# Routing tokens to expert slots by scatters and gathers of whole token rows, beside a sequential scan, on one Trainium2 core

## The chip, the cores and the metric

One core of one Trainium2 chip runs the whole program. The metric is the device time of one execution in microseconds, and less is better. The engines are TensorE (PE), VectorE (DVE), ScalarE (ACT), GpSimd (POOL) and SyncE (SP), which here only issues DMAs. A time comes from several runs; the profile is of one more execution.

## The reference

The input `x` is 4 sequences of 1024 tokens with 256 features, float32. After a layer norm, two branches read `xn`:

```python
# branch 1: a recurrence over the 1024 time steps, state h of (4, 256, 16)
dt = soft_clamp(softplus(xn @ Wdt.T + bdt), 0.001, 0.1, 0.5)
def step(h, inp):
    h = dAt * h + dBt * xt[..., None]
    h_norm = sqrt(sum(h * h, axis=(1, 2)))          # per sequence
    h = h * minimum(20.0 / (h_norm + 1e-08), 1.0)
    y = einsum('bdn,bn->bd', h, Ct) + Dp * xt
# branch 2: a mixture of 8 experts, top 2, capacity 1280 slots an expert
top_v, top_i = top_k(xn @ w_g, 2)
rank = cumsum(one_hot(top_i))                        # a token's place in its expert
keep = rank < 1280
exp_batches = einsum('tec,td->ecd', sec_mask, xn)    # token rows to their slots
exp_out = gelu(exp_batches @ c_fc) @ c_proj          # 256 -> 1024 -> 256
moe = cb_weight @ exp_out                            # back, weighted by softmax of the two
out = x + s * silu(moe)                              # s: output of branch 1
```

## The kernel before

**The scan.** DVE runs the 1024 steps one after the other, lines 778 to 811: the decayed state `vv` (L778), the clamp argument (L781), two reductions (L784, L792), a sum over partitions (L796), the new state `hr` (L807) and the recurrence of the norm (L811). In each step POOL takes one power (L554, `scale_of`) that L807 of the step needs and L781 has released. The state of all four sequences lies in one 128x128 tile a step.

**What feeds the scan.** Four steps are a quad, sixteen a block, 64 a half, so that a half is 16 quads. For each quad PE transposes four decay columns (L1227), ACT takes them out (L1009), PE spreads the inputs of four steps (L1231) and ACT takes these out with a scale (L1016). `da`, `ur` and `hr` are rings of 32 steps, so PE and ACT may run at most about two blocks ahead; they start a block when DVE has finished the block before the last. For each half ACT prepares the decays of the next: 32 tanhs (L912, `tanh_ops`, two a quad) and then four exponentials of 128x2048 (L919, `decay_ops`), which PE awaits at the head of a half (`decay_ready`). DVE also prepares input of later halves in pieces put between steps by the tables `sum_at` (`add_logs`, L637), `input_at` (`scan_input`, L645) and `norm_at` (L652). They are put one step behind a step with an indirect DMA (`delayed`), nine pieces a half.

**The experts.** 10240 slots are 40 tiles of 256, five an expert. A tile is one `turn` (four transposes of gathered rows), four `up` (8 matmuls each and one Gelu) and two `down` (16 each). A list `by_quad` spreads this work evenly over quads 1 to 231, by weights 1, 4 and 8. Rows of a tile are fetched from `xnd` in DRAM by two indirect gathers (L529) through the list `slot_src`, and its results are written to `moe` by two indirect scatters (L534) through `slot_dst`. POOL issues these at the steps of the table `at_step`, between two powers. ACT may overwrite `yrow` when POOL has seen the scatters land (`yrow_free`, a step of `freed_at`). From quad 240 on, PE combines: SP loads `moe` in token order (`load_pair`), ACT makes diagonal weights, PE adds the two rows and ACT takes the Silu.

**The prologue.** For eight tiles of the 4 x 128 tokens DVE normalizes; SP stores `xn` to `xnd`, `xn * Dp` to `dx` and the transposed tile to `xts`; PE makes the logits. `dxn` is a double buffer, so the tile after next waits for a store to `dx` to land. Then DVE works out experts, ranks and weights (L680 to L722), and one-hot products on DVE, POOL and PE invert the token-to-slot map into the slot lists (`one_hot`, `moe_rows`, `slots`, L731, L737, L520, L1146). The semaphore `loop_go` holds all engines until this is over:

```python
            pool.sem_inc(loop_go, 1)
            pool.wait_ge(loop_go, 5)
```

All of SP's DMAs stand in one queue, in order.

Of the kernel before, what the change touches and what calls it, by code (L numbers as in the profile page):

```python
# [20 lines left out]
P = 128  # L21
# [27 lines left out]
CONSTS = 22  # L49


def build(nc, x, wdtT, bdt, wb, wc, a_log, dpar, w_g, c_fc, c_proj, out):
# [4 lines left out]
    with ctx:  # L57
# [7 lines left out]
        xnd = nc.dram_tensor("xnd", (TOK + P, D), f32, kind="Internal").ap()  # L65

        moe = nc.dram_tensor("moe", (2 * TOK + P, D), f32, kind="Internal").ap()
# [21 lines left out]
        slot_src = sb("slot_src", [P, SC + EC], i32)  # L89
        slot_dst = sb("slot_dst", [P, SC], i32)  # L90
# [53 lines left out]
        def lay(n):  # L144
            at2[0] += n
            assert at2[0] <= 34688, at2[0]
            return arena[:, at2[0] - n:at2[0]]

        dxn = lay(2 * NB * D).rearrange("p (f b d) -> p f b d", f=2, b=NB)
# [21 lines left out]
        lo = lay(2 * JT).rearrange("p (k j) -> p k j", k=2)  # L171
        hi = lay(2 * JT).rearrange("p (k j) -> p k j", k=2)
        rank_i = lay(2 * JT).bitcast(i32).rearrange("p (k j) -> p k j", k=2)
        lo_i = lay(2 * JT).bitcast(i32).rearrange("p (k j) -> p k j", k=2)
        hi_i = lay(2 * JT).bitcast(i32).rearrange("p (k j) -> p k j", k=2)
        rowid = lay(2 * JT).rearrange("p (k j) -> p k j", k=2)
        rowid_i = lay(2 * JT).bitcast(i32).rearrange("p (k j) -> p k j", k=2)
        cols_i = lay(P).bitcast(i32)
        cols = lay(P)
        pcol = lay(1)  # L180
        acc = lay(SC)
        free = lay(SC)

        lohot = wp.rearrange("p k d -> p (k d)").rearrange("p (f n c) -> p f n c", f=2, n=8)
        wflat = wf.rearrange("p k d -> p (k d)")
        hihot = wflat[:, 0:8 * SC].rearrange("p (n c) -> p n c", n=8)
        hirow = wflat[:, 8 * SC:24 * SC].rearrange("p (f n c) -> p f n c", f=2, n=8)
        pw = lay(4 * JT).rearrange("p (k j) -> p k j", k=4)
        alog = lay(DH * NS)


# [56 lines left out]
        lo_ready = sem("lo_ready")  # L248
        hi_half = sem("hi_half")
        hi_ready = sem("hi_ready")  # L250
        hot_used = sem("hot_used")
        slots_ready = sem("slots_ready")
        loop_go = sem("loop_go")
# [31 lines left out]
        yrow_free = sem("yrow_free")  # L285
# [26 lines left out]
        QUADS, MOE_QUADS, COMBINE_AT = NT // QUAD, 232, 240  # L312
# [11 lines left out]
        at_step = {}  # L324
        for qd, items in enumerate(by_quad):
            for kind, i, j, _ in items:
                if kind == "turn" or (kind == "down" and j == 1):
                    for c in range(2):
                        k = max(2, qd * QUAD - QUAD) if c == 0 else k + (6 if kind == "down" else 1)
                        while k in at_step or k % BLK < 2:  # L330
                            k += 1
                        if kind == "down" or i + 1 < NE * TPE:
                            at_step[k] = (kind, i, c)

        freed_at = {k + 7: i for k, (kind, i, c) in at_step.items() if kind == "down" and c == 1}
        assert max(freed_at) < (COMBINE_AT - QPB) * QUAD and min(at_step) >= 0, (max(freed_at), min(at_step))
# [24 lines left out]
        def _(sp):  # L361
# [7 lines left out]
            sp.dma_start(xnd[TOK:TOK + P, :], zeros[:, 0:D]).then_inc(padz, 16)  # L369
            for b in range(NB):  # L370
                sp.dma_start(dx[0:YPAD, b, :], zeros[0:YPAD, 0:D]).then_inc(padz, 16)

            for i in range(CH):
                sp.wait_ge(xn_ready, i + 1)
                sp.dma_start(xnd[0:TOK, :].rearrange("(b i p) d -> p b i d", p=P, i=CH)[:, :, i, :], xnat[:, :, i, :]).then_inc(xn_out, 16)
# [11 lines left out]
            for i in range(CH):  # L387
                sp.dma_start(moe[i * NT:(i + 1) * NT, :].rearrange("(r p) d -> p r d", p=P),
                             zeros[:, 0:D].unsqueeze(1).broadcast_to([P, CH, D])).then_inc(moe_zero, 16)
            for k in range(2):  # L390
                sp.wait_ge(dx_done[k], 16 * CH // 2)
            sp.sem_inc(loop_go, 1)
            sp.wait_ge(padz, 16 * (NB + 1))
            sp.wait_ge(loop_go, 5)
            sp.sem_inc(y_out, 1)

# [9 lines left out]
            def load_pair(i):  # L406

                for k in range(2):
                    sp.dma_start(pair_in[i % 3][:, k], moe[k * TOK:(k + 1) * TOK, :].rearrange("(b i p) d -> p b i d", p=P, i=CH)[:, :, i, :])\
                        .then_inc(g_in[i % 3], 16)  # L410

            for blk in range(NBLK):
                load_dx(blk, span(blk * BLK, BLK))
                if blk in first_up:

                    m = first_up[blk]
                    if m == 0:
                        sp.wait_ge(hot_used, CH)
# [13 lines left out]
                if blk == COMBINE_AT // QPB - 1:  # L432

                    sp.wait_ge(ye_out, 32 * NE * TPE)
                    sp.wait_ge(norm_ready, HALVES)
                    for i in range(3):
                        load_pair(i)
# [28 lines left out]
        def _(pool):  # L466
# [57 lines left out]
            for i in range(CH):  # L524
                moe_rows(i)
# [232 lines left out]

# [559 lines left out]
```

## Time and profile before

| | us |
|---|---|
| three runs | 1732.36, 1732.87, 1743.9 |
| median | 1732.87 |
| profiled execution, its own time | 1741.31 |
| its span, first to last instruction | 1739.6 |
| mean granted TensorE clock | 0.88 of full |

The span lies 1.7 us below the execution's own time, and that execution is 8.4 us above the median. Shares of busy time are means over prologue, scan and end, which have different limits. A row of waits names the instruction that stood idle, and what released it.

### The profile page before, as it was taken

The page shows a single profiled execution, that of the slowest core. Times are in us where ns is not written, and L with a number is a line of the kernel's source. Part 1 is how long each engine was busy: PE and PEld are TensorE (multiplying, and loading weights), DVE is VectorE, ACT ScalarE, POOL GpSimd, SP SyncE. Part 2 cuts the span into 40 slices and gives each one's busy share as a digit, 9 for nine tenths or more (in the row PEclk, how much of TensorE's full clock was granted, in tenths as well). Part 3 has the DMA queues.
Part 4 walks back from the last instruction along what each step waited for, and adds up shares of the span by engine and source line. Part 5 has one row for each costly group of instructions (what it writes and reads, how often), then busy time and mean ns, then how long its engine had stood idle before and what let it go on. Part 6 is the DMA issues. An engine that isn't in the chain of part 4 may idle for free.

```text
span 1739.6 us, 34335 instructions
## 1 busy us (share of the span) xinstructions
PE 1312.5 (75%) x9480; PEld 1153.9 (66%) x9480; DVE 1583.9 (91%) x9554; ACT 1230.7 (71%) x3156; POOL 814.5 (47%) x1295
## 2 busy tenths in 40 slices
PE   5589797887868689877869689776959777764663
PEld 5478686776757578766758678666848666654552
DVE  7548999999989999999999999999999979999988
ACT  4628886869777677868778687958768595767452
POOL 4034554555445545554554554454545445444432
PEclk9559898898989889898989899898979988897886
DMA  9811001100101020101101110111001100003145
GB/s 314 283 60 38 18 28 58 41 23 22 63 24 35 19 68 26 34 22 41 50 19 35 44 50 19 34 44 44 25 16 50 44 19 23 13 16 97 63 151 198
DMA packets 77472, 98.64 MB, mean 57 GB/s; under 512 B 7776, under 2 KB 66272, under 8 KB 77280
## 3 DMA queue, kind: packets, MB, share of 16 engines
q1 hardware_dynamic: 68096, 75.25, 13.2%
q0 software_dynamic: 7680, 20.98, 3.7%
q8 instruction: 75, 1.23, 0.3%
q14 instruction: 117, 0.96, 0.2%
q10 hardware_dynamic: 1504, 0.22, 0.1%
HBM read 56.71 MB, written 39.71 MB: 55 GB/s over the span
## 4 chain that ended last, share of the span: by engine, by line
DVE 59%; POOL 18%; PE 10%; issue 7%; ACT 3%; SPq 1%; DMA 1%; POOLq 0%; DVEq 0%; ACTq 0%
DVE arena L807 13%; DVE arena L784 10%; DVE arena L796 9%; DVE arena L778 9%; POOL arena L554 8%; DVE arena L792 8%; DVE arena L811 6%; POOL moe L534 5%; POOL xrow L529 4%; DVE arena L781 3%; PE ps L1208 2%; PE ps L1146 2%; PE ps L1231 2%; PE ps L1227 1%; ACT arena L912 1%
## 5 line engine op out<-in xcount | busy, mean ns | idle before, releaser
L554 POOL TENSOR_TENSOR arena<-arena,neghalf 128x1 f32<-128x1 f32 x1025 | 592.0, 578 | 780.6 <-DVE arena L781 772.3
L807 DVE SCALAR_TENSOR_TENSOR arena<-arena 128x128 f32<-128x128 f32 x1024 | 363.4, 355 | 39.4 <-POOL arena L554 33.5
L1227 PE MATMUL ps<-ident,arena 128*128 128x128 f32 x1024 | 214.4, 337 | 227.7 <-ACT arena L919 159.6
L1227 PEld LDWEIGHTS ps<-ident,arena 128*128 128x128 f32 x1024 | 180.2, 244 | 269.0 <-ACT arena L919 164.5
L1243 PE MATMUL ps<-arena,wf 128*128 128x256 f32 x1280 | 311.7, 393 | 7.6 <-issue 7.6
L1016 ACT ACTIVATE arena<-ps,arena 128x128 f32<-128x128 f32 x1024 | 291.4, 376 | 25.2 <-PE ps L1231 24.2
L1231 PE MATMUL ps<-arena,pick 128*128 128x128 f32 x2048 | 296.7, 292 | 15.2 <-ACT arena L1016 15.2
L792 DVE CUSTOM_DVE_ANT_0 arena<-arena 128x128 f32<-128x128 f32 x1024 | 293.2, 286 | 9.3 <-ACT arena L1016 5.8
L784 DVE CUSTOM_DVE_ANT_0 arena<-arena 128x128 f32<-128x128 f32 x1024 | 299.1, 292 | 0.0
L1259 PE MATMUL ps<-wp,arena 128*128 128x256 f32 x1280 | 296.5, 386 | 0.2 <-ACT arena L1024 0.2
L778 DVE TENSOR_TENSOR arena<-arena 128x128 f32<-128x128 f32 x1024 | 290.7, 284 | 5.6 <-ACT arena L1016 5.6
L1231 PEld LDWEIGHTS ps<-arena,pick 128*128 128x128 f32 x2048 | 281.3, 212 | 19.3 <-ACT arena L1016 19.2
L796 DVE TRANSPOSE_TENSOR_REDUCE arena<-arena 128x2 f32<-128x64 f32 x1024 | 251.3, 245 | 35.5
L912 ACT ACTIVATE arena<-arena,a16c,a 128x256 f32<-128x256 f32 x512 | 279.8, 607 | 0.1
L1243 PEld LDWEIGHTS ps<-arena,wf 128*128 128x128 f32 x1280 | 245.3, 200 | 38.7 <-issue 8.5
L1259 PEld LDWEIGHTS ps<-wp,arena 128*128 128x128 f32 x1280 | 243.2, 195 | 30.8 <-ACT arena L1024 0.4
L811 DVE TENSOR_TENSOR_SCAN arena<-arena 128x2 f32<-128x2 f32 x1024 | 221.1, 216 | 0.0
L1009 ACT ACTIVATE arena<-ps 128x512 f32<-128x512 f32 x256 | 151.6, 592 | 68.5 <-PE ps L1227 68.4
L781 DVE TENSOR_SCALAR arena<-arena 128x1 f32<-128x1 f32 x1024 | 150.6, 147 | 0.0
L1024 ACT ACTIVATE arena<-ps 128x512 f32<-128x512 f32 x160 | 95.7, 606 | 52.6 <-PE ps L1243 49.1
L970 ACT ACTIVATE arena<-arena,winmask 128x16 f32<-128x16 f32 x520 | 110.8, 312 | 15.1 <-POOL arena L561 15.1
L919 ACT ACTIVATE arena<-arena 128x2048 f32<-128x2048 f32 x64 | 116.9, 1898 | 0.2
(158 smaller groups left out, 1406.2 us busy)
## 6 DMA issues: line engine op xcount, KB each, us to landing
arena<-in_x SPq DMA_DIRECT2D x16, 512.0 KB, 9.3
moe<-zeros SPq DMA_DIRECT2D x8, 1024.0 KB, 10.5
wf<-in_c_fc SPq DMA_DIRECT2D x8, 1024.0 KB, 5.0
wp<-in_c_proj SPq DMA_DIRECT2D x8, 1024.0 KB, 5.2
arena<-dx SPq DMA_DIRECT2D x66, 64.0 KB
ys<-arena SPq DMA_DIRECT2D x66, 64.0 KB
xnd<-arena SPq DMA_DIRECT2D x8, 512.0 KB, 5.4
dx<-arena SPq DMA_DIRECT2D x8, 512.0 KB, 5.6
```

Source lines behind the costliest of these rows:

```text
L554: g.tensor_tensor(sv[:, slot, 1:2], mx, neghalf[:, 0:1], ALU.pow).then_inc(s_ready, 1)
L778: v.tensor_tensor(vv, hr[:, before, :], da[:, slot, :], ALU.mult).then_inc(v_ready, 1)
L784: v.tensor_tensor_reduce(out=junk[:, 0, :], in0=vv, in1=ur[:, slot, :], scale=2.0 / CLAMP ** 2, scalar=0.0, op0=ALU.mult, op1=ALU.add, acc ...
L792: v.tensor_tensor_reduce(out=junk[:, 1, :], in0=vv, in1=vv, scale=1.0 / CLAMP ** 2, scalar=0.0, op0=ALU.mult, op1=ALU.add, accum_out=ac[:, ...
L796: v.tensor_reduce(out=terms[:, slot, 0:2], in_=ac.unsqueeze(2).broadcast_to([P, 2, 32]), axis=AX.X, op=ALU.add, apply_transpose=True).then ...
L807: v.scalar_tensor_tensor(hr[:, slot, :], vv, sv[:, before, 1:2], ur[:, slot, :], ALU.mult, ALU.add)\
L811: v.tensor_tensor_scan(horner, sv[:, before, 1:2].broadcast_to([P, 2]), terms[:, slot, 1:3], terms[:, slot, 0:1], ALU.mult, ALU.add).then_ ...
L912: last = a.activation(dst[:, :, k, n_, :], src[:, :, k, :], ACT.Tanh, scale=a16[:, c:c + 1], bias=a16c[:, c:c + 1])
L1227: last = t.transpose(ps[q % 2][:, j * P:(j + 1) * P], tanhb[:, f, :, s], ident[:, :])
L1231: last = t.matmul(ps[2][:, j * P:(j + 1) * P], pick[:, q * QUAD + j, :], xin, start=True, stop=True)
L1243: last = t.matmul(ps[4 + j % 2][:, c * TS:(c + 1) * TS], wf[:, k, (2 * j + c) * P:(2 * j + c + 1) * P], xt[:, k, :], start=k == 0, stop=k ...
L1259: last = t.matmul(ps[7][:, j * D:(j + 1) * D], hid[:, k, j * P:(j + 1) * P], wp[:, k, :], start=k == 0, stop=k == FC - 1)
```

## The change

Each token row is now sent to its expert slots, in place of a slot fetching its token.

- The slot lists, their one-hot work and `loop_go` are gone. DVE computes for each token and choice its slot number `slot_of` directly, or a spare row past the slots where the token is dropped.
- A DRAM tensor `xg` of 10240 + 128 rows is cleared in ten stores of 1 MB: eight of them go into SP's queue ahead of the eight tiles' own stores in the prologue, two behind them. (The eight 1 MB stores of zeros to `moe` are gone.)
- SP loads all token rows back from `xnd` into SBUF regions that are idle at that time (`homes`, seven loads). POOL sends them by 64 scatters of 128 rows at steps 12, 14, ... 138. Each one is issued only when the one before it has landed, and this wait stands ahead of the step's power.
- Experts read and write `xg` and `yg` by plain DMAs of SP, one a tile each way, issued when SP comes to the end of a block (`move_rows`). POOL has no indirect DMA from step 139 to 929.
- POOL fetches the results by 64 gathers at steps 930 to 993, one a step, straight into `pair_in`.
- Expert work is spread over quads 39 to 229 in place of 1 to 231. Combining starts at quad 237 in place of 240.
- DVE's pieces for later halves are wider and fewer: one `add_all_logs` over 128x512, two `half_scan_input` over 128x256 and one norm, a half.
- The `decay_ops` of a half come in quad 15 of 16 in place of that quad's two tanhs; the first half's decays are in four parts, the first ahead of the scan and the others in blocks 0 to 2. Input of half 2 is prepared in block 0.
- ACT goes into the scan when all stores to `xts` have landed, and POOL clears `hr` and `win` (4096 and 896 columns) after `route_ready`; DVE cleared `hr` before.

```diff
-        QUADS, MOE_QUADS, COMBINE_AT = NT // QUAD, 232, 240
+        QUADS, MOE_AT, MOE_QUADS, COMBINE_AT, LAST_HALF = NT // QUAD, 39, 230, 237, 240
...
-            by_quad[1 + (n + w[3] // 2) * (MOE_QUADS - 1) // total].append(w)
+            by_quad[MOE_AT + (n + w[3] // 2) * (MOE_QUADS - MOE_AT) // total].append(w)
...
+        SEND_AT, FETCH_AT = 12, 930
+        at_step = {SEND_AT + 2 * n: ("send", n) for n in range(2 * TILES)}
+        at_step.update({FETCH_AT + n: ("fetch", n) for n in range(2 * TILES)})
...
-            for table, pieces, lo_, hi_ in ((sum_at, 4, 4 * h - 9, 4 * h - 7), (input_at, 4, 4 * h - 6, 4 * h - 4), (norm_at, 1, 4 * h - 3, 4 * h - 1)):
-                lo_, hi_ = max(lo_ * BLK + 3, 2 + h % 2), hi_ * BLK
+            for table, pieces, lo_, hi_ in ((sum_at, 1, 4 * h - 9, 4 * h - 7), (input_at, 2, 4 * h - 6, 4 * h - 4), (norm_at, 1, 4 * h - 3, 4 * h - 1)):
+                lo_, hi_ = max(lo_ * BLK + 3, BLK + 2), max(hi_ * BLK, 2 * BLK)
...
+            def clear(i):
+                sp.dma_start(xg[i * NT:(i + 1) * NT, :].rearrange("(r p) d -> p r d", p=P),
+                             zeros[:, 0:D].unsqueeze(1).broadcast_to([P, CH, D])).then_inc(moe_zero, 16)
             for i in range(CH):
+                clear(i)
                 sp.wait_ge(xn_ready, i + 1)
...
+            def move_rows(kind, i):
+                if kind == "turn" and i == 0:
+                    sp.wait_ge(sent, 16 * 2 * TILES)
+                    sp.dma_start(xrow[:, :, :], xg[0:TS, :].rearrange("(c p) d -> p c d", p=P)).then_inc(xrow_in, 16)
+                if kind == "turn" and i + 1 < NE * TPE:
+                    sp.wait_ge(xt_tp, i + 1)
+                    sp.dma_start(xrow[:, :, :], xg[(i + 1) * TS:(i + 2) * TS, :].rearrange("(c p) d -> p c d", p=P)).then_inc(xrow_in, 16)
+                if kind == "down":
+                    sp.wait_ge(ye_sb, i + 2)
+                    sp.dma_start(yg[i * TS:(i + 1) * TS, :].rearrange("(c p) d -> p c d", p=P), yrow).then_inc(ye_out, 16)
...
+            def send(n):
+
+                j, k = divmod(n, 2)
+                first, home = homes[home_of(j)]
+                g.indirect_dma_start(out=xg, out_offset=bass.IndirectOffsetOnAxis(ap=slot_of[:, k, j:j + 1], axis=0),
+                                     in_=home[:, j - first, :], in_offset=None).then_inc(sent, 16)
...
+            g.memset(sv, 1.0).then_inc(init_win, 1)
+            pool.wait_ge(route_ready, 1)
+            g.memset(hr, 0.0).then_inc(h_ready, 1)
             g.memset(win, 0.0).then_inc(init_win, 1)
...
+                kind, n = at_step.get(step, ("", 0))
+                if kind == "send":
+                    if n == 0:
+                        pool.wait_ge(moe_zero, 16 * (SLOTS // NT))
+                    else:
+                        pool.wait_ge(sent, 16 * n)
+                    pool.wait_ge(tile_in[home_of(n // 2)], 16)
+                elif kind == "fetch":
+                    if n == 0:
+                        pool.wait_ge(padz, 16 * (NB + 1))
+                        pool.wait_ge(ye_out, 16 * NE * TPE)
...
+            hop(v.tensor_scalar(eix, eix, float(NE), float(CAP), ALU.add, ALU.mult))
+            hop(v.tensor_tensor(rank, rank, eix, ALU.add))
+            hop(v.scalar_tensor_tensor(rank, rank, nowhere, keep, ALU.subtract, ALU.mult))
+            hop(v.tensor_scalar(rank, rank, nowhere, None, ALU.add))
+            v.tensor_copy(slot_of[:, :, :], rank).then_inc(rt_in, 1)
             v.tensor_tensor(wsel[:, :, :], pw[:, 2:4, :], keep, ALU.mult).then_inc(route_ready, 1)
...
-                    if blk + 4 < NBLK:
+                    if blk + 4 < NBLK and quad % 16 < 15:
...
+                        first = 32 * (quad % 16) // 15
+                        last = tanh_ops(1 - f, first, 32 * (quad % 16 + 1) // 15 - first)
+                        if quad % 16 == 14:
+                            last.then_inc(tanh_done, 1)
+                    elif blk + 4 < NBLK:
+                        act.wait_ge(tanh_done, blk // 4 + 2)
+                        decay_ops(1 - f).then_inc(decay_ready, 1)
```

## Rows read from the trace of the kernel before

**Rows 1.** The page: span, busy time of the engines, one group of instructions.

```profile
span 1739.6 us, 34335 instructions
...
PE 1312.5 (75%) x9480; PEld 1153.9 (66%) x9480; DVE 1583.9 (91%) x9554; ACT 1230.7 (71%) x3156; POOL 814.5 (47%) x1295
...
L912 ACT ACTIVATE arena<-arena,a16c,a 128x256 f32<-128x256 f32 x512 | 279.8, 607 | 0.1
```

**Rows 2.** Timeline until the scan's first step: start us, us, engine.

```profile
1.53 1.81 POOL L477 MEMSET pick<- 128x2048 f32 x1
...
43.39 1.38 DVE L621 TENSOR_SCALAR arena<-arena,mv,rstd 128x256 f32<-128x256 f32 x4
...
54.41 18.61 SPq L388 DMA_DIRECT2D moe<-zeros  x8
...
56.96 0.29 DVE L680 CAST arena<-arena 128x256 f32<-128x256 int32 x1 [8.96 <-PE ps L1089]
...
64.27 0.42 DVE L696 COPY arena<-arena 128x512 f32<-128x512 f32 x1
...
72.74 0.69 DVE L705 COPY arena<-ps 128x512 f32<-128x512 f32 x1
...
79.82 0.22 DVE L722 TENSOR_TENSOR wsel<-arena 128x64 f32<-128x64 f32 x1
...
84.57 28.55 PE L1146 MATMUL ps<-wf,wp 128*128 128x80 f32 x128 [16.20 <-POOL wf L520]
...
125.17 0.29 DVE L778 TENSOR_TENSOR arena<-arena 128x128 f32<-128x128 f32 x1 [5.57 <-ACT arena L1016]
```

**Rows 3.** Stretches of the prologue; last: clock, DMA share, GB/s.

```profile
0.00:20.00 20.00, 3.72 (x17) 3.38 (x18) 11.64 (x42) 4.12 (x6) 12.23 (x30) 1.00 0.96 273
20.00:40.00 20.00, 18.66 (x177) 17.14 (x177) 19.50 (x67) 12.24 (x25) 4.99 (x4) 0.93 0.90 343
```

**Rows 4.** Timeline of POOL around one scatter inside the scan.

```profile
159.51 0.54 POOL L554 TENSOR_TENSOR arena<-arena,neghalf 128x1 f32<-128x1 f32 x1 [0.95 <-DVE arena L781]
160.24 1.14 POOL L534 DMA_INDIRECT moe<-arena,slot_dst  x1 [0.19 <-issue]
161.40 0.58 POOL L554 TENSOR_TENSOR arena<-arena,neghalf 128x1 f32<-128x1 f32 x1
```

**Rows 5.** Stretch without indirect DMAs, the first instruction of each step alone.

```profile
1566.60:1659.50 92.90, 18.14 (x64) 0.80 0.23 73
```

**Rows 6.** Waits of DVE, 209 to 1500 us: total, times, longest.

```profile
DVE arena L637 <- ACT arena L880: 14.9, 2, 7.6
```

**Rows 7.** The DMA view, indirect DMAs: count, us to landing.

```profile
xrow<-xnd,slot_src POOLq DMA_INDIRECT x80, 2.9
moe<-arena,slot_dst POOLq DMA_INDIRECT x80, 2.6
```

**Rows 8.** Groups of instructions, two DVE forms: busy us, mean ns.

```profile
L708 DVE TENSOR_TENSOR arena<-arena,ps 128x512 f32<-128x512 f32 x1 | 0.7, 686 | 0.0
...
L694 DVE SCALAR_TENSOR_TENSOR arena<-arena 128x256 f32<-128x256 f32 x1 | 0.4, 425 | 0.0
```

**Rows 9.** Waits of PE and ACT, 209 to 1500 us.

```profile
PE ps L1227 <- ACT arena L919: 138.2, 13, 14.5
ACT arena L1032 <- POOLq L582: 68.9, 11, 10.3
...
ACT arena L999 <- DVE arena L811: 33.2, 11, 5.8
```

**Rows 10.** Groups of instructions of PE, 209.2 to 1500.4 us.

```profile
L1243 PE MATMUL ps<-arena,wf 128*128 128x256 f32 x1152 | 282.1, 395 | 6.1 <-issue 6.1
L1259 PE MATMUL ps<-wp,arena 128*128 128x256 f32 x1152 | 266.5, 386 | 0.2 <-ACT arena L1024 0.2
...
L1227 PE MATMUL ps<-ident,arena 128*128 128x128 f32 x832 | 172.6, 334 | 193.7 <-ACT arena L919 138.2 <-ACT arena L961 55.5
```

**Rows 11.** PE's decay transposes, four a quad, while the kernel combines.

```profile
1590.40:1697.00 106.60, 13.42 (x56) 11.03 (x57) 0.84 0.30 94
```

More of the change, by code:

```diff
@@ L247, in build @@
         xn_out = sem("xn_out")
[L248 to L253, printed above, removed]
+        tile_in = [sem(f"tile_in{k}") for k in range(7)]
+        sent = sem("sent")
         init_win = sem("init_win")
@@ L386, in _, with load_rows @@
             load_chunk(1)
-            for i in range(CH):
-                sp.dma_start(moe[i * NT:(i + 1) * NT, :].rearrange("(r p) d -> p r d", p=P),
-                             zeros[:, 0:D].unsqueeze(1).broadcast_to([P, CH, D])).then_inc(moe_zero, 16)
+            def load_rows(n):
+                first, home = homes[n]
+                count = home.shape[1]
+                sp.dma_start(home, xnd[first * P:(first + count) * P, :].rearrange("(j p) d -> p j d", p=P)).then_inc(tile_in[n], 16)
+            sp.wait_ge(padz, 16 * (NB + 1))
+            sp.sem_inc(y_out, 1)
+            sp.dma_start(dxt, dx[0:BLK, :, :].rearrange("t b (k d) -> (t b k) d", k=DH)).then_inc(dx_in, 16)
+            for i in range(CH, SLOTS // NT):
+                clear(i)
             for k in range(2):
                 sp.wait_ge(dx_done[k], 16 * CH // 2)
[L392 to L395, printed above, removed]
+            sp.wait_ge(xn_out, 16 * CH)
+            load_rows(0)
+            load_rows(1)
+            sp.wait_ge(route_ready, 1)
+            for n in range(2, 6):
+                load_rows(n)
             def load_dx(n, at):
@@ L431, in _ @@
                 store_y(blk, span(blk * BLK, BLK))
[L432 to L437, printed above, removed]
-                for i in {COMBINE_AT // QPB: (3,), COMBINE_AT // QPB + 1: (4, 5), COMBINE_AT // QPB + 2: (6, 7)}.get(blk, ()):
-                    sp.wait_ge(comb_ps, 2 * (i - 2))
-                    load_pair(i)
+                if blk == 3:
+                    sp.wait_ge(sent, 16 * 4)
+                    load_rows(6)
+                for kind, i in moved[blk]:
+                    move_rows(kind, i)
                 if blk == NBLK - 2:
-                    sp.wait_ge(ta_ps, COMBINE_AT + 1)
+                    sp.wait_ge(ta_ps, LAST_HALF + 1)
                     for i in range(CH):
@@ L580, in _ @@
                     scaled_c(1 - step // BLK % 2, ccol[:, span(step, BLK)], step + 1 + BLK, step // BLK + 1)
-                if step in freed_at:
-                    pool.sem_inc(yrow_free, 1)
-                if step in at_step:
-                    kind, i, c = at_step[step]
-                    if kind == "turn":
-                        gather(c, slot_src[:, 2 * (i + 1) + c:2 * (i + 1) + c + 1])
-                    else:
-                        scatter(c, slot_dst[:, 2 * i + c:2 * i + c + 1])
+                if kind == "send":
+                    send(n)
+                elif kind == "fetch":
+                    fetch(n)
             scale_of(RING - 1, NT + 1 + BLK)
@@ L653, in norm_of_input @@
                     .then_inc(norm_ready, 1)
+            for s_, c_ in ((T_ready, BLK), (v_ready, BLK), (ac_ready, BLK), (m_ready, BLK), (h_ready, BLK), (q_ready, BLK)):
+                dve.sem_inc(s_, c_)
+            v.memset(qv, 1.0).then_inc(q_ready, 1)
             statistics(0)
@@ L696, in _ @@
             v.tensor_copy(ohb, ohf).then_inc(rt_in, 1)
+            for h in range(2):
+                norm_of_input(h)
             dve.wait_ge(gap_exp, 1)
@@ L913, in tanh_ops, with decay_op @@
                 return last
+            def decay_op(f, c):
+                part = tanhb[:, f, :, c * BLK:(c + 1) * BLK]
+                a.activation(part, part, ACT.Exp, scale=16.0).then_inc(decay_ready, 1)
             def decay_ops(f):
@@ L1131, in _ @@
                 last = logits(i)
-            last.then_inc(lg_ps, 1)
-            for h in range(2):
-                sums_of_squares(h, PREP_BANKS[h])
+                if i == CH - 1:
+                    last.then_inc(lg_ps, 1)
+                if i >= CH - 2:
+                    sums_of_squares(i - (CH - 2), PREP_BANKS[i - (CH - 2)])
             pe.wait_ge(rt_in, 1)
```

275 lines of the change are left out of this document (97 added, 178 removed).

## The prediction

> **What bounds the kernel now.** I read the page first: DVE is busy 91% of the span, PE 75% [rows 1]. The shares are means over three stages, so the timeline comes next. The scan's first step starts at 125.2 us [rows 2]; all before it is prologue, where DVE works half the time. In the scan, a stretch without indirect DMAs has 64 steps in 92.9 us, 1.45 us a step [rows 5], and this is a loop between DVE and POOL: DVE's clamp argument, POOL's power, DVE's new state. Whatever POOL does between two powers lengthens the step. The timeline of POOL shows it: with a scatter between, two powers start 1.89 us apart (159.51, 161.40) and not 1.45 [rows 4]. An indirect DMA costs the scan 0.44 us, and there are 160 [rows 7]: 70 us. Third, who else can hold the scan: in DVE's waits two pieces for a later half waited 14.9 us in all for ACT's logarithm [rows 6]. Last, how much slack PE and ACT have. In the 1291.2 us from 209.2 to 1500.4, PE made 832 decay transposes, 208 quads or 13 halves, 99.3 us a half [rows 10]. ACT stood 68.9 us for POOL's word that `yrow` is free, which comes at a fixed step, and 33.2 us for DVE to end a block [rows 9]. Both waits are for the scan itself, so they are slack: 102.1/13 = 7.9 us a half. Fed at once, PE and ACT together would make a half in about 91.4 us. That number decides most of what follows.
>
> **The prologue.** `wsel` is at 79.8 us [rows 2]. What stands between it and the first step, 45.3 us, is the one-hot inversion (28.6 us of matmuls from 84.6 on), the lists, the first gathers, clearing `hr` and the first quad. The change removes nearly all of this, but puts 8 MB of zeros ahead of the stores on which DVE's double buffer waits. Rate: 343 GB/s from 20 to 40 us, with the DMA engines 90% busy already, and 273 x 20 = 5.5 MB moved by 20 us [rows 3]. A tile then takes a clear of 1.05 MB and three stores of 0.52 MB: 2.62 MB at 345 GB/s is 7.6 us, where DVE needs about 4.5 us for its own work. By 20 us some 4.8 MB are the first loads and pads, so the sixth store to `dx` (number 5) ends when 19.5 MB are moved, 60.6 us, and number 4 at 53. Number 4 frees the buffer for tile 6, and the normalization of tile 7 follows it: about 56, ready at 57.7, where it began at 43.4 [rows 2]. PE then has a transpose group, two groups of logits and one of squares at the lower clock, some 10 us (estimate), so DVE reads the logits at 67 to 68, where it began at 57.0. From there to the one-hot masks it took 7.3 us (57.0 to 64.3, plus 0.4); four small casts now lie ahead, so 6.7. The masks were copied by 64.7 and the ranks read at 72.7 [rows 2]; of these 8 us I give 3.6 to PE's two 512-column products (estimate) and the rest to ACT's exponential, which stood behind its tanhs. The tanhs now come earlier, so I take that wait at 0 (ends 0 and 4). The rank chain took 7.1 us to `wsel` (72.7 to 79.8 [rows 2]); it loses three or four hops of about 0.23, leaving 6.5. Sum: 67.8 + 6.7 + 3.6 + 6.5 = 84.6. Then POOL clears `hr`: 2048 columns took 1.81 us [rows 2], so 4096 take 3.6, and 0.9 for `win`: 90 us. ACT and PE are not later: the last `xts` store lands when 25.2 MB are moved, 77 us, plus a landing, and the first quad needs some 5 us. The first step also waits 2 us for PE's output product, which it did too in smaller measure. So **the scan starts at 90 us in place of 125: -35**. If the clears did not hold DVE, the same chain gives 79, -46; if clears and rest run at 273 GB/s, 105, -20.
>
> The Trainium skill (DMA: Bandwidth & Descriptors, Queues, rings and completion order) says that descriptors of one issuing engine's ring are consumed in ring order and that only queues of different rows take turns. By this the clears do hold back the stores behind them, as I assume; no row here has stores behind clears. The nearest row agrees that SP's queue fills up: its eight stores of zeros at 54.4 us took 18.6 us only to be issued [rows 2].
>
> **Indirect DMAs in the scan.** 160 become 128, each at 0.44 with POOL as before: **-14**. A gather in every step from 930 costs the same, since the powers would be 1.89 apart.
>
> A new wait: a scatter waits for the one before it, and the power of its step and with it all of DVE wait behind. From the start of the scatter to the power two steps on is 1.89 + 1.45 - 0.73 = 2.61 us, and a scatter's median landing is 2.6 [rows 4, 7]. So it fits with nothing to spare. I take 0.05 a scatter, **+3**; ends 0 and, with the gathers' 2.9 for each plus a semaphore's time, 63 x 0.5 = +32.
>
> The Trainium skill (DMA: Bandwidth & Descriptors, Anatomy of one DMA) gives a fixed cost of about 2.0 us, mostly the write's receipt, plus bytes at 436 GB/s: an estimate of 2.3 us for these 131 KB, under which the wait would be nothing. The rows say 2.6 and decide.
>
> **DVE's pieces.** They sat in steps lengthened by a DMA and cost nothing. Now only halves 2, 3 and part of 4 find such steps. A 128x512 add takes 0.69 and a 128x256 one 0.43 [rows 8]; a plain step has about 0.1 us of room. So 11 x 0.6 + 24 x 0.33 + 12 x 0.08 = **+15**. Ends 8 and 20.
>
> **Stalls that go.** The two of 14.9 us [rows 6] came when a half's preparation stood behind a turn that waited for POOL; in both the scan stood for it. Nothing waits for POOL there now: **-15**. Late next is PE, below.
>
> **Denser expert work.** `by_quad` now has 191 quads in place of 231, 21% more a quad. Expert matmuls were 282.1 + 266.5 = 548.6 us, 42.2 a half [rows 10], so +8.8. Off comes one: the decays no longer follow two tanhs at 0.6 [rows 1], and PE awaits them at each half (138.2/13 = 10.6 us [rows 9]), -1.1. I take another -1.5 for dips of the clock that the scan-paced waits cause and for turns that waited on gathers. Half: 91.4 + 8.8 - 1.1 - 1.5 = 97.6 us. DVE, freed of DMAs, makes a half in 64 x 1.45 = 92.9 plus 1.3 of pieces, 94.2. So **PE and ACT become the bound in the expert quads**, by 3.4 us a half. The ring covers the first losses: at a block's start DVE may be 32 steps (46 us) from needing what comes after the decays, and PE needs two to three quads, the wait and the first slow quad, some 38: 8 us of cover. Twelve halves end in the expert stretch: 11 x 3.4 - 8 = **+30**. Ends: 0 if a half takes 95 or less; +75 at 101.7.
>
> A second rule of the Trainium skill (TensorE: Matmul & The Clock Gate, Part 1) is that idleness throttles PE and activity releases it. It speaks for the lower end, since a denser PE would have fewer half-speed stretches; the mean clock here is 0.88 and no row separates the two uses of it.
>
> **The end.** While it combines PE needs 106.6/14 = 7.6 us a quad [rows 11], above DVE's 5.8. The combines now lie on quads 237 to 252, of which twelve have gathers in the steps and run at 7.6. The lead is less strained but capped by the gathers' landing at about two quads. I take the same stalls as before, 0, with +-8.
>
> **Sum.** -35 - 14 + 3 + 15 - 15 + 30 = -16. Against the profiled execution's 1741.3 (span 1739.6 and 1.7) this is 1725; that one lay 8.4 above the median of the runs, 1732.9, and I forecast for the median: **1717 us**.
>
> **Rivals.** (a) PE keeps up: fewer half-speed stretches take a half of PE and ACT to 94 or less. Then the 30 fall away: 1687. For it: a fifth of the quads' work is done faster at full clock than my mean price. Against: the wait for the decays remains at each half. (b) PE and ACT are far behind, the case on the other side: in place of POOL's DMAs the scan waits in each half for its decays. Place: steps after each half's start; price 11 times the excess; it is slower by 1% once a half needs 100.6 us (3 more than mine, which is +33, and so 1750). At 102 it gives 1765. For it: 91.4 + 8.8 without my deductions is 100.2. Against: DVE would have to see none of the waits shrink. (c) Scatters land late, since loads and chunk traffic share the engines: +0.8 each over 63 is +50, 1764. For: the window equals the median. Against: SP's large loads are over before step 12. (d) The clears don't hold DVE: start at 79, 1706. (e) The change doesn't shorten the prologue as it says, because the clears push everything to 105 us: 1732.
>
> **How the numbers follow.** A measurement here can't tell less than about 1% (17 us) from no change. My case has 0.40, and with its bounds lies at 1700 to 1738, somewhat under half of it below 1715.6. (a) 0.24, (d) 0.08, (b) 0.13, (c) 0.07, (e) 0.08. Faster by over 1%: 0.17 + 0.24 + 0.07 = 0.48. Slower by over 1% (above 1750.2): 0.11 from (b) and 0.06 from (c) = 0.17. The rest, 0.35, is within 1%. For 8 in 10 the range must take in most of (a) and the near part of (b): 1680 to 1752. The chance is on the faster side, so my case's own range, 1700 to 1738, stands beside it.
>
> **What would show it.** The scan's first step at 80 to 95 us, and normalizations about 7.6 us apart. The 64 sends: powers 1.89 and 1.45 apart in turn; longer ones show (c). Steps with pieces 0.3 to 0.6 longer. In the expert quads the sign is DVE idle before L778 or L792 for ACT's `ur` or PE's output, growing from the fourth or fifth half on; if DVE has no such wait, (a) holds. ACT's waits for POOL and for the end of a block should have gone from these halves if PE is the bound. I would be wrong outright if a wait on SP's queue (expert weights behind `sent`, `dx` rows behind `move_rows`) held PE for long.

## The result, and the profile after

The change makes the kernel slower: 1766.53 us, median of 4 runs (1763.11 to 1767.62), against 1732.69, median of 4 runs, for the kernel before; ratio 1.0154, 95% interval 1.0115 to 1.0193. The forecast was 1717, with 1680 to 1752 as its range. The profiled execution took 1766.3 us (span 1764.2; before 1741.31 and 1739.6 [rows 1]). So 24.6 us of span were lost where 16 were expected to be gained. One run of the last experiment below, of 1941.08 us, was in a slower state of the chip and is not in its ratio.

The page after: span, busy time, one row of the slices (44.1 us each), one group.

```profile
span 1764.2 us, 33864 instructions
...
PE 1302.9 (74%) x9352; PEld 1143.0 (65%) x9352; DVE 1550.5 (88%) x9455; ACT 1227.6 (70%) x3152; POOL 770.1 (44%) x1254
...
DVE  6588888888979998997989899998989799997778
...
L863 ACT ACTIVATE arena<-arena,a16c,a 128x256 f32<-128x256 f32 x512 | 278.5, 609 | 0.1
```

All engines are busy for less time than in [rows 1], and the span is longer: a wait was added, no work. First the start, to be compared with [rows 2]:

```profile
21.19 1.38 DVE L602 TENSOR_SCALAR arena<-arena,mv,rstd 128x256 f32<-128x256 f32 x4
...
48.71 1.37 DVE L602 TENSOR_SCALAR arena<-arena,mv,rstd 128x256 f32<-128x256 f32 x4
53.41 1.36 DVE L602 TENSOR_SCALAR arena<-arena,mv,rstd 128x256 f32<-128x256 f32 x4
...
60.82 0.29 DVE L676 CAST arena<-arena 128x256 f32<-128x256 int32 x1
...
75.44 0.69 DVE L703 COPY arena<-ps 128x512 f32<-128x512 f32 x1 [2.76 <-PE ps L1110]
...
82.07 0.22 DVE L716 TENSOR_TENSOR wsel<-arena 128x64 f32<-128x64 f32 x1
...
82.35 3.51 POOL L527 MEMSET arena<- 128x4096 f32 x1 [32.16 <-DVE wsel L716]
85.80 0.84 POOL L528 MEMSET arena<- 128x896 f32 x1
...
86.81 0.29 DVE L727 TENSOR_TENSOR arena<-arena 128x128 f32<-128x128 f32 x1 [4.52 <-POOLq L531]
```

The stores behind the clears do hold DVE back (last normalization at 53.41, not 43.39), and the scan still starts 38.4 us earlier, at 86.81. The same stretch as in [rows 3] shows the DMA engines full, and faster than before (386 GB/s against 343; last columns clock, DMA share, GB/s):

```profile
20.00:40.00 20.00, 18.20 (x161) 16.26 (x160) 14.58 (x51) 11.74 (x27) 3.74 (x3) 0.85 1.06 386
```

The scan's last step starts 25.8 us ahead of the end of the span (1738.35 to 1764.2; before 26.0). So from the start of the first step to the start of the last the scan took 1651.5 us, where it took 1588.4. The length of each step can be read from the starts of L727, the first instruction of a step. Sends and fetches lengthen a step by 0.44 and 0.42, as before. The rest is in the waits, here of 350 to 1500 us, to be compared with [rows 6, 9]:

```profile
PE ps L1179 <- ACT arena L875: 107.8, 12, 9.0
DVE arena L623 <- ACT arena L829: 70.1, 11, 10.3
ACT arena L990 <- PE ps L1213: 64.7, 28, 2.8
...
ACT arena L954 <- DVE arena L760: 29.6, 14, 4.8
```

The second row is new in size: 70.1 us in 11 waits, where [rows 6] had 14.9 in 2. L623 is the wide add of ACT's logarithm (L829). ACT's wait for POOL in [rows 9] is gone, and its wait for a block's end (L954) is still there. One of the eleven, in DVE's timeline:

```profile
497.64 0.25 DVE L745 TRANSPOSE_TENSOR_REDUCE arena<-arena 128x2 f32<-128x64 f32 x1
506.10 0.69 DVE L623 TENSOR_TENSOR arena<-arena 128x512 f32<-128x512 f32 x1 [8.22 <-ACT arena L829]
506.71 0.35 DVE L756 SCALAR_TENSOR_TENSOR arena<-arena 128x128 f32<-128x128 f32 x1
```

and ACT at that time (L875: the decays, L822 and L824: relu and absolute value, L829: the logarithm):

```profile
494.64 7.31 ACT L875 ACTIVATE arena<-arena 128x2048 f32<-128x2048 f32 x4
...
502.92 0.48 ACT L824 ACTIVATE arena<-ps,arena 128x256 f32<-128x256 f32 x1
504.08 1.28 ACT L829 ACT_TABLE_LOAD   x1
505.37 0.63 ACT L829 ACTIVATE arena<-arena 128x512 f32<-128x512 f32 x1
```

The scan stands still, with all its inputs there, because a piece of work for a half that starts some 140 steps later was put into step 3 of block 4h-9 (blocks 11, 15, ... 51), and ACT makes the logarithm for it at the end of its own block 4h-9, behind four decays of 7.3 us together. By the rings ACT can be at most about two blocks ahead of DVE. Here it was less than one block ahead (DVE is in step 3 of block 15 at 497.64, and ACT ends its own block 15 at 506.0), so DVE gets to the piece first. Before, the free steps were those behind an indirect DMA, and mostly these lay later in the block.

### The profile page after: what moved, and what is told of

Same layout as the page of the kernel before. It is cut to its first block, busy times and chain, and to the rows that moved or that the text cites. A ratio compares the mean times of both kernels' runs of the same rounds, so it can differ in the third digit from the quotient of the medians.

```text
span 1764.2 us, 33864 instructions
## 1 busy us (share of the span) xinstructions
PE 1302.9 (74%) x9352; PEld 1143.0 (65%) x9352; DVE 1550.5 (88%) x9455; ACT 1227.6 (70%) x3152; POOL 770.1 (44%) x1254
## 4 chain that ended last, share of the span: by engine, by line
DVE 47%; PE 23%; ACT 9%; issue 8%; POOL 8%; DMA 3%; POOLq 0%; SPq 0%; DVEq 0%; ACTq 0%
DVE arena L756 10%; DVE arena L733 8%; DVE arena L745 7%; DVE arena L741 7%; DVE arena L727 7%; DVE arena L760 4%; PE ps L1213 4%; PE ps L1197 4%; POOL arena L536 4%; ACT arena L875 4%; PE ps L1185 4%; POOL xg L515 3%; PE ps L1160 3%; PE ps L1179 2%; DVE arena L730 2%
## 5 line engine op out<-in xcount | busy, mean ns | idle before, releaser
L1185 PE MATMUL ps<-arena,pick 128*128 128x128 f32 x2048 | 306.7, 298 | 39.5 <-ACT arena L971 20.1
L1185 PEld LDWEIGHTS ps<-arena,pick 128*128 128x128 f32 x2048 | 285.1, 214 | 51.3 <-ACT arena L971 38.2
L971 ACT ACTIVATE arena<-ps,arena 128x128 f32<-128x128 f32 x1024 | 292.2, 377 | 35.1 <-PE ps L1185 34.7
L1197 PE MATMUL ps<-arena,wf 128*128 128x256 f32 x1280 | 302.8, 387 | 8.1 <-issue 8.1
L727 DVE TENSOR_TENSOR arena<-arena 128x128 f32<-128x128 f32 x1024 | 289.9, 283 | 4.5 <-POOLq L531 4.5
L1197 PEld LDWEIGHTS ps<-arena,wf 128*128 128x128 f32 x1280 | 241.1, 195 | 39.0 <-issue 9.3
L1140 PE MATMUL ps<-arena,ident 128*128 128x128 f32 x132 | 34.8, 351 | 153.6 <-ACT arena L925 140.6
L925 ACT ACTIVATE arena<-arena,winmask 128x16 f32<-128x16 f32 x520 | 111.0, 312 | 40.4 <-POOL arena L543 40.2
```

The source lines that it names most:

```text
L727: v.tensor_tensor(vv, hr[:, before, :], da[:, slot, :], ALU.mult).then_inc(v_ready, 1)
L971: last = a.activation(ur[:, t + j, :], ps[2][:, j * P:(j + 1) * P], ACT.Copy, scale=terms[:, t + j, 3:4])
L1185: last = t.matmul(ps[2][:, j * P:(j + 1) * P], pick[:, q * QUAD + j, :], xin, start=True, stop=True)
L1197: last = t.matmul(ps[4 + j % 2][:, c * TS:(c + 1) * TS], wf[:, k, (2 * j + c) * P:(2 * j + c + 1) * P], xt[:, k, :], start=k == 0, stop=k ...
```

## The experiments

Eleven kernels ran. Each ratio is to the kernel before on the same chip, whose medians there were 1743.34 (the first four), 1741.13 (the next four) and 1742.98 (the last three). So ratios are compared, and times only within a group. The kernel before itself varies more than the others: from 1731.49 to 1747.99 over all its runs, where the runs of each other kernel agree within 0.5%. A difference of two ratios from different groups carries that.

**The position of the wide add.** In the changed kernel the add goes one block later:

```diff
-            ... ((sum_at, 1, 4 * h - 9, 4 * h - 7), ...
+            ... ((sum_at, 1, 4 * h - 8, 4 * h - 7), ...
```

> The changed kernel with one edit: DVE's one add of a half's logarithms stands one block later (block 4h-8 in place of 4h-9, again its step 3). Theory A, a latency loop: in the changed kernel DVE meets this add at step 3 of the same block at whose end ACT takes the logarithms, behind the decays; the 12 waits of 4 to 11 us (83 us) are that loop and nothing else, so they go and nothing takes their place: about 1766 - 80 = 1686 us, halves of about 94 us. Rival B, density (my prediction's step): PE and ACT need about 98 us a half with 21% more expert work, so a wait of some 4 us a half comes back at the ring (DVE's first instruction or its reductions waiting for ACT or PE): 1766 - 83 + 30 to 45 = 1715 to 1728 us.

Measured: 1720.0 us, ratio 0.9856 (0.9837 to 0.9875). One number in a table turns 1.5% slower into 1.4% faster. In time it is 46.5 us (medians; 46.3 between the two spans); the ratios lie 3.0 points apart because the kernel before was slower in this group (1743.34 against 1732.69). The steps say the same: those with an add take 71.4 us less together, those with an input piece 26.3 more. So not all of the add's wait was won, and the time came out where rival B had it (1715 to 1728), not at theory A's 1686, though with a wait that B did not name. In the waits of 350 to 1500 us no add is left; what stands there now is the input piece at step 3 of nine blocks:

```profile
PE ps L1179 <- ACT arena L875: 107.9, 12, 9.0
...
DVE arena L629 <- ACT arena L833: 30.5, 9, 7.5
```

**The same in the kernel before, in both directions.** The chunked adds of later halves in the first steps from step 3 of block 4h-9 on, without looking for delayed steps:

```diff
-                chosen = sorted((free_ + spare)[:pieces])
+                chosen = sorted(free_ + spare)[:4] if table is sum_at and h >= 3 else sorted((free_ + spare)[:pieces])
```

> The kernel before with one edit: the four adds of a half stand at the first four free or delayed steps of their two blocks in order of time, from step 3 of block 4h-9 on, in place of the delayed steps first. Density, gathers and the prologue are those of before. Theory A: the same wait appears in every half, as in the two halves of before where the first add already stood at step 3 (7.6 and 7.8 us): 11 more of 5 to 8 us, plus 0.15 for each add at a plain step, so 1733 + 60 to 90 = 1793 to 1823 us. Rival B: PE and ACT are fast enough at the old density, so the position costs only the 0.15 for each add: 1735 to 1745 us.

Measured: 1800.9, ratio 1.0326 (1.0305 to 1.0348). The add's wait, 14.9 us in [rows 6], is now 58.0 in 10, and the time lies where theory A had it:

```profile
DVE arena L637 <- ACT arena L880: 58.0, 10, 11.8
```

And one block later:

```diff
-            ... ((sum_at, 4, 4 * h - 9, 4 * h - 7), ...
+            ... ((sum_at, 4, 4 * h - (8 if h >= 3 else 9), 4 * h - 7), ...
```

> The kernel before with one edit: the four adds of a half from the third on stand one block later (blocks 4h-8 alone). Theory A: the two waits of 14.9 us go, with perhaps 1 to 3 us for adds that no longer find a delayed step: 1719 to 1722 us. My prediction's reading, that both stalls came from a turn waiting for POOL's gathers: they stay, 1733 to 1737 us.

Measured: 1732.59, ratio 0.9936 (0.9917 to 0.9955). With nothing of the change in it, the kernel before gains 0.6% and the waits of [rows 6] are gone; between the two traces the span falls by 9.3 us (1739.6 to 1730.3). Elsewhere three of four runs of the kernel before were at 1732.4 to 1732.9 without this edit, so the waits gone from the trace say more than the 0.6%. In the trace of the kernel before one of the two waits is at an add in step 3 of block 15:

```profile
509.08 0.29 DVE L637 TENSOR_TENSOR arena<-arena 128x128 f32<-128x128 f32 x1 [7.35 <-ACT arena L880]
```

So the position alone, without sends, density or wide pieces, makes the kernel before 3.3% slower at one place, and at another takes its two waits away.

**The clears.** All ten go behind the tile stores in SP's queue:

```diff
-                clear(i)
...
-            for i in range(CH, SLOTS // NT):
+            for i in range(SLOTS // NT):
```

> The changed kernel with all ten clears of xg behind the stores of the eight tiles, none ahead. If the clears hold DVE's double buffer as predicted, tiles are normalized about 4.5 to 5.3 us apart again and not 5.3 to 7.4, the last one some 9 us earlier, and the scan's first step comes 5 to 9 us earlier (86.8 to about 79): 1758 to 1762 us, if the sends at step 12 do not wait for the clears. Rival: the clears then end only when the sends should start (10 MB at 345 GB/s from about 60 us on, and 2 MB of rows behind them: 98 us or later) and step 12 (about 97 us) waits for them: no gain, 1764 to 1770 us.

Measured: 1762.7, ratio 1.011 (1.009 to 1.013); the first step is at 83.18, 3.6 us earlier, and the median falls by 3.8. This lies between the two expectations (1758 to 1762, and 1764 to 1770). DVE's last normalization comes 5.4 us earlier (47.97 in place of 53.41), but then DVE waits for PE's logits:

```profile
61.33 0.42 DVE L679 COPY arena<-ps 128x256 f32<-128x256 f32 x1 [10.13 <-PE ps L1058]
```

In the changed kernel that wait is 3.5 us. From 40 to 60 us PE was granted 0.50 of its clock in both, the lower of its two levels (1.2 GHz), and with the clears behind it is busy for all of these 20 us. So the clears do hold DVE, but they cost 3.6 us of the start, not the 11 between 90 and 79, because PE comes next.

**Both kinds of piece later.** On top of the later add, the input pieces begin at step 11 of their block for halves 4 and up:

```diff
-                lo_, hi_ = max(lo_ * BLK + 3, BLK + 2), ...
+                lo_, hi_ = max(lo_ * BLK + (11 if table is input_at and h >= 4 else 3), BLK + 2), ...
```

> The kernel of e1 with DVE's two input pieces of a half half a block later (step 11 of block 4h-6 in place of 3; from half 4 on). In e1 nine of these waited 2 to 8 us, 35 us in all, for ACT's tanh at the end of its own block 4h-6: the same loop as with the add. Theory A, only the loops: they go and nothing comes back, e1 - 30 to 35 us, 1685 to 1690 us. Rival B, density: PE and ACT need about 98 us a half, so most of it comes back as DVE waiting for the ring or for PE's output: e1 - 0 to 15, 1705 to 1720 us.

Measured: 1716.72, ratio 0.987 (0.9811 to 0.9929), no different from the add alone, and where rival B had it. (Ten halves, from block 11 to block 51, take 96.3 us each, and 96.2 with the add alone.) Waits of DVE, 350 to 1500 us:

```profile
DVE arena L741 <- ACT arena L971: 23.9, 11, 3.5
```

No piece waits any more. What DVE waits for is `ur` (L971), mostly in step 15 ahead of a half. Two halves of the expert region, stretch by stretch (PE, PEld, DVE, ACT, POOL; clock, DMA share, GB/s):

```profile
575.20:672.70 97.50, 85.63 (x623) 75.54 (x622) 91.81 (x582) 78.34 (x199) 38.02 (x68) 0.95 0.16 47
672.70:770.20 97.50, 83.98 (x610) 74.03 (x610) 91.81 (x582) 76.09 (x197) 38.02 (x68) 0.95 0.11 36
```

With the pieces out of the way PE and ACT set the pace, at 97.5 us a half. Eight halves take 96.8 in the mean, two of them 94.0 and 94.4, near DVE's own 94.2 in the prediction. For PE and ACT the prediction had 97.6. Taking the input's waits away gave nothing measurable because DVE then catches up with this pace: the wait changed its place.

**Denser still.** The expert work of that kernel on quads 39 to 204:

```diff
-        QUADS, MOE_AT, MOE_QUADS, COMBINE_AT, LAST_HALF = NT // QUAD, 39, 230, 237, 240
+        QUADS, MOE_AT, MOE_QUADS, COMBINE_AT, LAST_HALF = NT // QUAD, 39, 205, 237, 240
```

> e6 with the expert work on quads 39 to 204 (166 quads) in place of 39 to 229 (191): 15% denser again, about 7.7 us more of PE in a half. If a half of PE and ACT takes 98 us in e6 (rival B), it takes some 105 here against DVE's 94: 10 halves by 11 less the cover, e6 + 55 to 70 us. If it takes 92 or less (theory A), it is 99 here and only 10 x 5 less the cover shows: e6 + 20 to 35 us.

Measured: 1798.58, ratio 1.0332 (1.0269 to 1.0396), 82 us more than without. The same wait grows:

```profile
DVE arena L741 <- ACT arena L971: 81.0, 14, 11.7
```

This is 191 quads' work on 166, 15% more a quad. By the prediction's price (42.2 us of expert matmuls a half before, 51.0 with the change) that is 7.7 us a half. Measured over ten halves, from block 11 to block 51, it is 8.5: 104.8 us a half against 96.3. So density costs its full price once PE and ACT set the pace.

**The kernel before, dense.** Its expert work on quads 39 to 231 in place of 1 to 231:

```diff
-            by_quad[1 + (n + w[3] // 2) * (MOE_QUADS - 1) // total].append(w)
+            by_quad[39 + (n + w[3] // 2) * (MOE_QUADS - 39) // total].append(w)
```

> The kernel before with its expert work on quads 39 to 231 in place of 1 to 231 and nothing else changed: density alone, with the gathers, scatters and the narrow pieces of before. By my prediction's arithmetic a half of PE and ACT goes from 91.4 to about 99 us, and DVE's from 97 to 98 (12 indirect DMAs a half): before + 0 to 20, by waits at the adds of later halves, since ACT is later at the end of its blocks. If density were the main cause of the slowdown of the whole change, it would show here as + 60 or more.

Measured: 1785.82, ratio 1.0266 (1.0203 to 1.0328). Of DVE's waits those of the pieces grew, from 14.9 to 54.9 us together, and the time by 44.7. ACT's wait for POOL hardly did (68.9 before):

```profile
ACT arena L1032 <- POOLq L582: 71.4, 12, 11.9
...
DVE arena L637 <- ACT arena L880: 38.3, 8, 9.7
...
DVE arena L645 <- ACT arena L884: 16.6, 6, 6.6
```

The 44.7 us lie between the expectations: above the 0 to 20 of the arithmetic, below the 60 at which density would have been the main cause. In this kernel density costs nearly as much as the early adds did, and through the same waits. The reading is that density takes away ACT's lead, and that a piece that stands too early is the first to feel it. It is not tested: neither this kernel with its adds later, nor the changed kernel with its early add at the old density, was run.

**Decays in four parts in every half.** PE waits 107.8 us for the decays at the heads of halves in the changed kernel, and 107.9 in the one with both kinds of piece later. In the latter each block now makes its own quarter (the edit also makes PE wait for one quarter a block):

```diff
-                        decay_ops(1 - f).then_inc(decay_ready, 1)
-                    if q == 2 and blk < 3:
-                        decay_op(0, blk + 1)
+                        decay_op(1 - f, 0)
+                    if q == 2 and blk % 4 < 3:
+                        decay_op(f, blk % 4 + 1)
```

> e6 with the decays of every half in four parts of 16 steps, as the changed kernel does for the first half alone: the first part in quad 15, the others in the third quad of blocks 0 to 2 of the half, PE waits for one part a block. PE's wait of about 9 us at each half falls to 3 or 4; ACT loads its tables some six times more a half (+8 us busy). Rival B (PE and ACT set the pace of a half): 12 x 3 to 5 us off, e6 - 20 to 45. Theory A (DVE sets it): e6 +- 5.

Measured: 1758.09, ratio 1.0106 (1.0046 to 1.0167): 41 us worse than without, which both expectations missed. The loads of ACT's function tables, 400 to 1450 us, are these:

```profile
L979 ACT ACT_TABLE_LOAD x42 | 53.9, 1283 | 9.2 <-PE ps L1194 8.6
L869 ACT ACT_TABLE_LOAD x41 | 52.6, 1283 | 0.3
```

where the kernel with whole decays has these:

```profile
L979 ACT ACT_TABLE_LOAD x11 | 14.1, 1283 | 3.1 <-PE ps L1197 3.0
L875 ACT ACT_TABLE_LOAD x10 | 12.8, 1283 | 0.2
```

62 more loads of 1.283 us are 80 us of ACT, between Gelu and the decays' exponential, and ACT was half of the pair that set the pace. PE's wait for the decays did fall, to 59.2 us (350 to 1500), but another took its place, for ACT's copy of the inputs (L917), which was 12.2 us before the split:

```profile
PE ps L1182 <- ACT arena L917: 67.2, 35, 3.3
PE ps L1176 <- ACT arena L869: 59.2, 24, 3.6
```

That the loads are what made it slower was not tested by itself.

**PE's wait filled.** PE does the up and down products of a half's first quad ahead of its wait for the decays: first in the kernel with both kinds of piece later, then there with the clears behind as well, and last in the changed kernel with its early add:

```diff
+                if blk * QPB % 16 == 0:
+                    for kind, i, j, _ in by_quad[blk * QPB]:
+                        if kind != "turn":
+                            expert(kind, i, j)
                 if blk < 4:
                     pe.wait_ge(decay_ready, blk + 1)
```

> The kernel with both sets of pieces later, and TensorE does the up and down products of the first quad of each half before it waits for the decays instead of behind them. Theory, that PE and ACT in turn set the pace of a half (96.8 us against DVE's 94.2 before) and that PE's 9 us wait for the decays is part of that turn: the wait holds about 3 us of expert work, so each of 11 halves is up to 2.6 us shorter, down to DVE's own 94.2: 20 to 29 us below 1716.7, about 1692. Rival, that ACT alone is the bound there: what PE does in its wait is hidden, 1717, 5 either way. Second rival, that the expert items delay ACT, which evicts them, behind the decays: slower by up to 10.

> The same and all ten clears of the slots behind the tile stores, which started the scan at 83.18 instead of 86.81. If the pace behind the start is set by the halves, the start is a lead that is kept to the end only as far as PE and ACT start earlier too: 3.6 us below the kernel without it, or 0 if PE and ACT set the end. In the changed kernel alone it gave 4 us.

> The changed kernel with the early add and only the fill of PE's wait. Theory of the loop (DVE's step 3 of every fourth block waits for ACT's logarithms, which stand at ACT's end of the block): PE's saving reaches the time only as far as it moves ACT's end of a block forward; at most 2.6 us of each of 11 waits of 4 to 11 us, so 1740 to 1766, with the add's waits on ACT still there, 40 us or more together. Rival, that PE's rate and not the position of the add is what costs: the waits go and the time falls to 1700 or below.

Measured: 1721.78, ratio 0.9869 (0.9848 to 0.9891); 1719.08, ratio 0.9867 (0.9844 to 0.9889); 1765.9, ratio 1.0126 (1.0096 to 1.0156). PE's wait did shrink, from 107.9 us (350 to 1500) to

```profile
PE ps L1216 <- ACT arena L875: 76.8, 12, 9.0
...
PE ps L1140 <- ACT arena L925: 31.6, 15, 3.0
DVE arena L741 <- ACT arena L971: 30.9, 13, 5.6
```

and nothing came of these 31 us. PE did not keep them: it now waits 31.6 us for ACT's `win` (L925), where it waited 6.0, so that its waits together shrank by only 8 us. The theory that PE's wait is part of the pace falls. The rival, that ACT's chain ends last, agrees with it. The third expectation, up to 10 us slower, is not excluded either (5 us between the medians of two groups). In the third kernel the add waits as ever:

```profile
DVE arena L623 <- ACT arena L829: 67.7, 11, 10.1
```

The clears show as 2.7 us between the first two medians, with a first step that comes 2.8 us earlier (84.10, 86.93); this is less than these runs can tell. The kernels with both pieces moved, with or without this, are about 1.3% faster than the kernel before and not told apart from each other or from the one with the add alone.

## Why the prediction was wrong

**Start: right.** -35 forecast, -38.4 seen. The chain held link by link: the last normalization at 53.41 (56 forecast), the logits read at 65.01 (67 to 68), `wsel` at 82.07 (84.6), `hr` in 3.51 us (3.6). The price of the clears was 3.6 us and not 11, as moving them showed: rival (d) took the logits at their old time, 57.0, and without the clears ahead of the stores they were read at 61.33, held by PE.

**Indirect DMAs: right.** 128 at 0.44 and 0.42. The new wait of a scatter for the one before it was put at +3, with an end at +32. It is there, in POOL's waits of 86 to 350 us:

```profile
POOL arena L536 <- DMA xg<-arena,slot_of: 24.2, 23, 1.9
POOL arena L536 <- DMA xg<-wf,slot_of: 20.7, 18, 2.5
POOL arena L536 <- DMA xg<-wp,slot_of: 14.8, 15, 1.5
POOL arena L536 <- DMA xg<-xrow,slot_of: 4.6, 4, 1.7
```

So 60 of the 63 powers that could wait for a scatter were released, by the profile, by its landing. Mostly this comes just behind the usual time:

```profile
124.90 1.12 POOL L515 DMA_INDIRECT xg<-wf,slot_of  x1 [0.17 <-issue]
126.06 0.56 POOL L536 TENSOR_TENSOR arena<-arena,neghalf 128x1 f32<-128x1 f32 x1
127.57 0.54 POOL L536 TENSOR_TENSOR arena<-arena,neghalf 128x1 f32<-128x1 f32 x1 [0.95 <-DMA xg<-wf,slot_of]
```

From send to power it is 2.67 here and in the median, against the 2.61 that were worked out, so 0.06 a scatter where 0.05 was forecast. Nine took 3.0 to 4.4 us, and with them the 63 come to some 11 us. Rival (c), +50, did not happen, but its mechanism is there at a fifth of its price.

**Pieces: their own time right, their place missed.** An input piece added 0.38 to 0.40 (0.33 forecast), the wide add 0.55 where it did not wait (0.6 forecast). The term of +15 priced a piece as work and never asked what it waits for.

**"Stalls that go" is the step that failed.** It said that the two stalls of 14.9 us [rows 6] came when a half's preparation stood behind a turn that waited for POOL, and that both would go: -15. [rows 6] name L637 waiting for L880, nothing more; the turn was my guess. The step numbers would have told: the two steps, longer by 7.62 and 7.85 us, are step 3 of block 15 and step 5 of block 51. In every other block 4h-9 from block 11 on the first add stood at step 9 or later, or in the next block. The change puts every add at step 3, since from step 139 to 929 there is no step with an indirect DMA for it to stand behind. The eleven steps with the wide add are longer by 77.4 us together, and step 3 of block 10, with an input piece, by 5.6: 83.0 in place of 15.5, which is +67.5 where the prediction had -15. Moving the add alone took 46.5 us off, against the 49.5 by which the median missed the forecast; the rest of the 71.4 us that its steps lost came back at the input pieces, and with these moved too, as DVE's wait for `ur`.

**Denser work: the half right, the rest hidden.** With the pieces later a half takes 96.3 to 97.5 us, near the 97.6 that were worked out, and DVE's wait for ACT's `ur`, the sign that was named, is there with 23.9 us; the term was +30. In the changed kernel itself this pace did not set the time: halves took about 100 us, of which the add's wait was a part. Rival (b) had the right sign, and its 1765 is the measured time by luck: its place was "steps after each half's start", where the long steps are step 3 of a half's last block, and its mechanism, PE and ACT past 100.6 us a half by their own work, did not happen. Without the early add they make a half in 97.

**Sum.** Over 1.45 us a step, the 1024 steps, the last one taken to its end, lost 168.3 us in the changed kernel and 105.2 before, +63.1. The indirect DMAs are -15.7 of it (64 at 0.44 and 64 at 0.415 against 160 at 0.44), the long steps +67.5, and all the rest +11.3 by difference. In that rest are the scatters' wait, some 11, and the other pieces' own time in steps without a DMA, some 10; so smaller losses of before fell by some 10, which were not followed further. With the start's -38.4 and 0.2 less behind the last step this is the 24.6 us of the span. Against the prediction: start -35 and -38; DMAs -14 and -16; scatters' wait, pieces and all small losses +18 and +11; stalls and density together +15 and +67. The ratio of the kernel with both pieces later, 0.987, gives 1710 on the median of before, its own median is 1716.72, and with the failed step so removed the forecast of 1717 would have stood.

## What to carry to other kernels

When side work is placed between the steps of a bound loop, its price is its duration plus any wait for its input, and that input comes from another engine whose lead over the loop may be small: one wide add of 0.69 us cost 70.1 us of waits at step 3 of eleven blocks, and none one block later. Ask for each piece how far ahead its producer can be at most, by the rings and buffers, and put the piece at the end of its window unless something needs it early. Attribute a stall of before by the step in which it stands, not by a story about its neighbours: two waits of 7.5 us at the earliest places of a table were a warning for all eleven. Where two engines in turn set a pace, filling the idle time of one can do nothing, as it did here: look first at what its work behind the wait will wait for next. And here the split of a batch of one function added 77 table loads, with 41 us of time.

## What the runs showed of the hardware

A switch of ACT's function table took 1283 ns in every kernel here, with the next activation starting at once (load at 493.34, exponential at 494.64). The Trainium skill (ScalarE: Activation LUTs, What ACT_TABLE_LOAD costs) adds a drain of about 1.38 us to it; the trace does not show one at that place. The kernel with the split decays has 128 loads in all where the one without has 51. It is 41 us slower, which is 0.54 us for each of the 77 more, if the loads are all that made the difference.

The DMA engines moved 386 GB/s while stores of zeros stood between loads and tile stores, 12% more than in [rows 3] (318 in the same stretch with the clears behind the stores). The mean share of the window is given as 1.06, so that column can pass 1.
